# Two layer norms share their logarithm, exponential and shift, and the attention norm is applied on ScalarE instead of VectorE

## The reference

```python
h   = layernorm(x)                                # norm of x, no gamma
q   = h @ Wq.T + bq ; k, v = ctx @ Wk.T + bk, ctx @ Wv.T + bv
att = h + (q @ (k.T @ v, block by head)) / 4      # attention residual
x1  = x + layer_norm(att) * gamma + beta
h2  = layernorm(x1)                               # norm of x1
w, e = top2(softmax(h2 @ gate_w.T))
out = x1 + sum_i w_i * relu(h2 @ expert_w[e_i].T + expert_b[e_i])
```

## Time and profile before

| | |
|---|---|
| median of 3 runs | 878.47 us (875.46 to 879.29) |
| the profiled execution | 878.41 us, span 876.6 us |
| busy share of the span | PE 86%, DVE 78%, ACT 68%, POOL 67% |
| dense half, roughly | start to 478 us |
| expert half | 478 us to the end |

### The profile page before, as it was taken

The page is one execution under the profiler, slowest core; times in us unless marked ns, Lnnn a source line. Parts: engine busy times, 40 slices in busy tenths (PEclk is TensorE's granted clock), DMA queues, the critical chain, the costliest instruction groups (busy, mean ns, idle before and its releaser), DMA issues. The chain is left out here.

```text
span 876.6 us, 21081 instructions
## 1 busy us (share of the span) xinstructions
PE 754.3 (86%) x5513; PEld 658.7 (75%) x5514; DVE 684.4 (78%) x2226; ACT 592.4 (68%) x1660; POOL 590.6 (67%) x776
## 2 busy tenths in 40 slices
PE   5988899999999999999998877788768899877850
PEld 4866688888888888888884777787756799767750
DVE  4999999999999999999995766777763566555540
ACT  4877789989998998899982545555542567554540
POOL 4578766666666666666664667777675577777775
PEclk9999999999999999999999999999999999999985
DMA  7526456666667667667612889999986999999941
GB/s 226 175 69 176 143 181 215 213 228 227 203 231 234 202 221 236 212 204 233 225 45 86 284 295 305 308 303 305 317 278 226 312 402 373 326 313 306 309 170 73
DMA packets 137628, 205.79 MB, mean 235 GB/s; under 512 B 38962, under 2 KB 74290, under 8 KB 137546
## 3 DMA queue, kind: packets, MB, share of 16 engines
q1 hardware_dynamic: 113101, 130.72, 47.4%
q0 software_dynamic: 24448, 74.14, 22.9%
HBM read 87.99 MB, written 116.81 MB: 234 GB/s over the span
## 5 line engine op out<-in xcount | busy, mean ns | idle before, releaser
L627 POOL DMA_INDIRECT bins<-row_in,put_at x143 | 139.3, 974 | 61.0 <-issue 47.7
L627 POOL DMA_INDIRECT out_rows<-xh,put_at x143 | 138.9, 971 | 56.1 <-issue 37.7
L607 POOL DMA_INDIRECT bins<-rows x128 | 126.6, 989 | 71.0 <-POOL rows L600 47.5
L697 PE MATMUL ps_q<-h_t,wq 128*128 128x256 f32 x512 | 131.6, 379 | 0.0
L556 POOL TENSOR_TENSOR c_rest<-c_sb,c_head 128x240 fp32r<-128x240 f32 x64 | 44.4, 694 | 86.8 <-DVE x L1157 82.2
L697 PEld LDWEIGHTS ps_q<-h_t,wq 128*128 128x128 f32 x512 | 91.7, 189 | 13.2 <-ACT h_t L942 0.4
L990 ACT ACTIVATE ps_q<-ps_q,row_in 128x256 f32<-128x256 f32 x144 | 58.5, 444 | 56.8 <-PE ps_q L826 55.4
L824 PE MATMUL ps_q<-we_head,row_head 128*128 x288 | 87.9, 305 | 8.6 <-DVE row_rest L1288 8.5
L901 ACT ACTIVATE q_t<-ps_q,bq_sb 128x256 f32<-128x256 f32 x128 | 60.4, 472 | 34.5 <-PE ps_q L697 34.5
L571 POOL TENSOR_TENSOR x_beta<-xh,beta_sb 128x512 f32<-128x512 f32 x64 | 81.9, 1280 | 0.8 <-DVE x L1157 0.8
L825 PE MATMUL ps_q<-we_head,row_rest 128*128 x288 | 81.5, 283 | 0.0
(11 more groups left out here) (178 smaller groups left out, 2413.2 us busy)
## 6 DMA issues: line engine op xcount, KB each, us to landing
bins<-zeros SPq DMA_DIRECT2D x48, 768.0 KB, 4.6
row_in<-bins SPq DMA_DIRECT2D x128, 260.0 KB
row_in<-bins SPq DMA_DIRECT2D x160, 132.0 KB, 2.1
xh<-in_x SPq DMA_DIRECT2D x64, 256.0 KB, 2.7
c_sb<-in_ctx_t SPq DMA_DIRECT2D x64, 120.0 KB, 3.3
we<-in_we_t SPq DMA_DIRECT2D x8, 512.0 KB, 6.9
bins<-row_in,put_at POOLq DMA_INDIRECT x143, 3.7
out_rows<-xh,put_at POOLq DMA_INDIRECT x143, 4.6
```

The lines of the kernel that those rows point to most:

```text
L607: pool.indirect_dma_start(out=bins[0], in_=r[:, t, :], out_offset=bass.IndirectOffsetOnAxis(ap=r[:, t, POS_COL:POS_COL + 1].bitcast(I32), ...
L627: pool.indirect_dma_start(out=bins[1] if k == 0 else out, in_=row_in[:, t, :] if k == 0 else y[:, t, :], out_offset=bass.IndirectOffsetOnA ...
L697: mm = pe.matmul(ps_q[dc][:, 0:S], wq[:, c, dc * P:(dc + 1) * P], h_t[:, c, :, :], start=(c == 0), stop=(c == KC - 1))
```

## The change

The logarithms and exponentials of the norm of x (batch s+1) and of the attention residual (batch s-1) become one logarithm and one exponential on ScalarE (`inverse_roots_x_att`), which wait for both sets of moments. VectorE makes both shifts in one instruction (`mean_shifts`). ScalarE applies the norm to the attention residual, one instruction per tile (`normalise_attention`), and stands for that ahead of the copy of h2. VectorE then multiplies both tiles by gamma in one instruction and adds `x_beta` to both in one (`scale`, `finish_x1`); `scale` moves from ahead of the mask to the end of the step. The shift of the norm of x1 moves from two instructions on ScalarE to one on VectorE, between the top values and their indices.

```diff
-            def shift_of_x1(b):
-                act.wait_ge(s_rstd[2], b.times(1, 1))
...
-                for t in range(NT):
-                    a = act.activation(rows[:, b.buf(4), t, S_COL:S_COL + 1], st[:, 2, b.buf(2), t, 1:2], ACT.Identity,
-                                       bias=sigma[:, t:t + 1], scale=-1.0)
...
+            def inverse_roots_x_att(s):
+                norms, n = norms_of(s)
+                if (s + 1).exists():
+                    act.wait_ge(s_mv[0], (s + 1).times(1, 1))
+                if (s - 1).exists():
+                    act.wait_ge(s_mv[1], (s - 1).times(1, 1))
+                act.activation(lnv[:, norms], st[:, norms, n, :, 2], ACT.Ln, bias=eps[:, 0:1],
+                               scale=1.0 / D).then_inc(s_ln["x_att"], 1)
+                act.wait_ge(s_ln["x_att"], s.times(1, 2))
+                act.activation(rstd[:, norms, n, :], lnv[:, norms], ACT.Exp, scale=-0.5).then_inc(s_rstd["x_att"], 1)
+
+            def normalise_attention(b):
+                act.wait_ge(s_shift["x_att"], b.times(1, 3))
+                if b.c >= 1:
+                    act.wait_ge(s_x1, (b - 1).times(NT, NT))
+                for t in range(NT):
+                    a = act.activation(scaled[:, t, :], att[:, t, :], ACT.Identity,
+                                       bias=nmr[:, 1, t:t + 1], scale=rstd[:, 1, b.buf(2), t:t + 1])
+                a.then_inc(s_z, 1)
...
+            def mean_shifts(s):
+                norms, n = norms_of(s)
+                dve.wait_ge(s_rstd["x_att"], s.times(1, 2))
+                dve.scalar_tensor_tensor(out=nmr[:, norms], in0=st[:, norms, n, :, 1], scalar=-1.0,
+                                         in1=rstd[:, norms, n, :], op0=ALU.mult, op1=ALU.mult
+                                         ).then_inc(s_shift["x_att"], 1)
+
+            def shift_of_x1(b):
+                dve.wait_ge(s_sigma, b.times(1, 1))
+                if b.c >= 4:
+                    dve.wait_ge(s_row[b.buf(4)], (b - 4).uses(4, 32))
+                dve.tensor_tensor(rows[:, b.buf(4), :, S_COL], sigma[:], st[:, 2, b.buf(2), :, 1],
+                                  ALU.subtract).then_inc(s_shift["x1"], 1)
...
-                dve.wait_ge(s_mv[1], b.times(1, 1))
-                for t in range(NT):
-                    i = dve.scalar_tensor_tensor(out=scaled[:, t, :], in0=att[:, t, :],
-                                                 scalar=st[:, 1, b.buf(2), t, 1:2], in1=gamma_sb[:],
-                                                 op0=ALU.subtract, op1=ALU.mult)
-                i.then_inc(s_scaled, 1)
+                dve.wait_ge(s_z, b.times(1, 1))
+                dve.tensor_tensor(scaled[:], scaled[:], gamma_sb[:].unsqueeze(1).to_broadcast([P, NT, D]),
+                                  ALU.mult).then_inc(s_scaled, 1)
...
-                for t in range(NT):
-                    dve.scalar_tensor_tensor(out=x1[:, b.buf(2), t, :], in0=scaled[:, t, :],
-                                             scalar=rstd[:, 1, b.buf(2), t:t + 1],
-                                             in1=x_beta[:, b.buf(2), t, :], op0=ALU.mult,
-                                             op1=ALU.add).then_inc(s_x1, 1)
+                dve.tensor_tensor(x1[:, b.buf(2)], scaled[:], x_beta[:, b.buf(2)], ALU.add).then_inc(s_x1, NT)
```

More of the change, by code:

```diff
@@ L217, in build @@
         sigma = sb("sigma", [P, NT])
-        nmr = sb("nmr", [P, NT])
+        nmr = sb("nmr", [P, 2, NT])
         scores_top = sb("scores_top", [P, NT, E + 8])
@@ L300, in build @@
         s_mv = [sem(f"moments{n}_ready") for n in range(3)]
-        s_ln = [sem(f"log_var{n}_ready") for n in range(3)]
-        s_rstd = [sem(f"rstd{n}_ready") for n in range(3)]
-        s_nmr = {0: sem("shift0_ready"), 2: sem("shift2_ready")}
+        s_ln = {"x_att": sem("log_vars_x_attention_ready"), "x1": sem("log_var_x1_ready")}
+        s_rstd = {"x_att": sem("rstds_x_attention_ready"), "x1": sem("rstd_x1_ready")}
+        s_sigma = sem("sigma_x1_ready")
+        s_shift = {"x_att": sem("shifts_x_attention_ready"), "x1": sem("shift_x1_ready")}
+        s_z = sem("attention_normalised")
         s_h = sem("h_ready")
@@ L363, in batch_of, with norms_of @@
             return view[b.c]
+        def norms_of(s):
+            return slice(0 if (s + 1).exists() else 1, 2 if (s - 1).exists() else 1), (s + 1).buf(2)
         def pieces(step, each):
@@ L883, in _, with inverse_root_x1 @@
             act.activation(wkv_head[:], wkv, ACT.Copy).then_inc(s_wkvh, 1)
[L885 to L893, removed]
+            def inverse_root_x1(b):
+                act.wait_ge(s_mv[2], b.times(1, 1))
+                act.activation(lnv[:, 2, :], st[:, 2, b.buf(2), :, 2], ACT.Ln, bias=eps[:, 0:1],
+                               scale=1.0 / D).then_inc(s_ln["x1"], 1)
+                act.wait_ge(s_ln["x1"], b.times(1, 1))
+                act.activation(sigma[:], lnv[:, 2, :], ACT.Exp, scale=0.5).then_inc(s_sigma, 1)
+                act.activation(rstd[:, 2, b.buf(2), :], lnv[:, 2, :], ACT.Exp, scale=-0.5).then_inc(s_rstd["x1"], 1)
+            def inverse_roots_x_att(s):
[16 more added lines that the diff above has]
+                a.then_inc(s_z, 1)
             def copy_q(b, dc):
@@ L908, in gate_exps @@
                 act.activation(exps[:], gaps[:], ACT.Exp).then_inc(s_exp, 1)
-            def shift_of_x1(b):
-                act.wait_ge(s_rstd[2], b.times(1, 1))
-                if b.c >= 4:
-                    act.wait_ge(s_row[b.buf(4)], (b - 4).uses(4, 32))
-                for t in range(NT):
-                    a = act.activation(rows[:, b.buf(4), t, S_COL:S_COL + 1], st[:, 2, b.buf(2), t, 1:2], ACT.Identity,
-                                       bias=sigma[:, t:t + 1], scale=-1.0)
-                a.then_inc(s_nmr[2], 1)
             def shift_x1(b):
-                act.wait_ge(s_nmr[2], b.times(1, 1))
+                act.wait_ge(s_shift["x1"], b.times(1, 1))
                 for t in range(NT):
@@ L928, in normalise_x @@
             def normalise_x(b):
-                act.wait_ge(s_nmr[0], b.times(1, 1))
+                act.wait_ge(s_shift["x_att"], b.times(1, 1))
                 if b.c >= 4:
@@ L934, in normalise_x @@
                     a = act.activation(h[:, b.buf(4), t, :], x_sb[:, b.buf(4), t, :], ACT.Identity,
-                                       bias=nmr[:, t:t + 1], scale=rstd[:, 0, b.buf(2), t:t + 1])
+                                       bias=nmr[:, 0, t:t + 1], scale=rstd[:, 0, b.buf(2), t:t + 1])
                 a.then_inc(s_h, 1)
@@ L952, in step @@
                 if b.exists():
-                    inverse_root(2, b)
+                    inverse_root_x1(b)
                 if s.exists():
@@ L956, in step @@
                 if b.exists():
-                    shift_of_x1(b)
                     shift_x1(b)
-                if nxt.exists():
-                    inverse_root(0, nxt)
+                if nxt.exists() or p.exists():
+                    inverse_roots_x_att(s)
                 if f.exists():
@@ L963, in step @@
                 if p.exists():
-                    inverse_root(1, p)
+                    normalise_attention(p)
                 if b.exists():
@@ L1196, in step @@
                     top_values(f)
+                if b.exists():
+                    shift_of_x1(b)
                 if f.exists():
@@ L1211, in step @@
                     add_kv_bias(s)
-                if nxt.exists():
-                    mean_shift(0, nxt)
+                if nxt.exists() or p.exists():
+                    mean_shifts(s)
                 if f.exists():
                     pick_ranks(f)
-                if p.exists():
-                    scale(p)
-                if f.exists():
                     sum_exps(f)
@@ L1225, in step @@
                     first_weights(f)
+                if p.exists():
+                    scale(p)
                 if f.c == NB - 1:
```

1 line of the change is left out of this document (removed).

## The result

The changed kernel takes 922.0 us (median of 4 runs, 921.58 to 922.57); the kernel before, beside it on the same chip, takes 878.9 (875.46 to 880.0, 4 runs). The ratio is 1.0498, interval 1.0468 to 1.0528: **slower by 43 us**, where 919 was forecast. The profiled execution's span is 919.8 us against 876.6.

What follows compares the result with a forecast made beforehand. VectorE was taken to pace the dense half at 6.64 us a step. Terms -0.35 + 0.39 + 0.02 + 0.09 + 0.50 gave about 0.64 a step; 31.4 + 6.8 + 2.4 = 40.6 on 878.4 gave 919 us, range 892 to 927.

Steps and rivals of the forecast that it cites:

- case A: Whole kernel: the prediction's main case, all its terms as summed, 919 us, own range 908 to 925; chance 0.77.
- the weight steps and the ends: Dense half: seven steps with `we` work lose 0.97 each, 6.8 us; eight end steps 0.3 each, 2.4 us.
- the even steps: Middle of the dense half: 49 steps, each 0.64 us longer, 31.4 us in all.
- The shift is held: VectorE, dense step: the shift of x1, two SBUF inputs, is blocked until GpSimd's `x_beta` ends, +0.39 us a step.
- The late shared `rstd`: Dense step: VectorE waits after `kv` for ScalarE's shared logarithm and exponential, which need the attention's moments; +0.09 us.
- The hole in front of `kvm`: VectorE, dense step: with the scaled pair moved away, `kvm` waits idle for `ps_mg`, +0.50 us.
- The merged pairs: VectorE, dense step: two `scaled` and two `x` become two 512-column instructions of 0.69 us; -0.35 us a step.
- ScalarE hidden, 0.14 to spare: Dense step: ScalarE's normalisation runs from 4.62 to 5.70, is needed at 5.84, and adds no time.
- case D: Dense half: ScalarE becomes the pace, gate and attention late, 0.1 to 0.15 us a step above A, 926; chance 0.07.
- B: Dense half: the shift is not held, 0.23 us a step over 64 steps, 893 us; chance 0.09.
- C: Dense half: no hold and `kvm` does not wait, -0.26 us a step over 62 steps, 862 us; chance 0.04.
- E: Whole kernel: no change, as B with a hole of only a third, 880 us; chance 0.03.

Runs made afterwards that it cites:

- e1: The changed kernel with sigma kept in PSUM, so the shift of x1 reads one input from SBUF; 900.0 us, ratio 1.0248.
- e2: The kernel before with only the shift of x1 moved to VectorE, both inputs in SBUF; 899.7 us, ratio 1.0258.
- e3: The kernel before with only the shift of x1 moved to VectorE and sigma in PSUM; 880.1 us, ratio 1.0018.
- e6: The changed kernel with GpSimd's `x_beta` moved behind the scatters, sigma still in SBUF; 976.8 us, ratio 1.1123.
- e7: The kernel before with the row of expert numbers that `onehot` compares with kept in PSUM; 879.6 us, ratio 1.0026.
- e4: e1 with the attention norm back on VectorE in pairs and old places, logarithm, exponential and shift still shared; 891.0 us, ratio 1.0137.
- e5: e1 with the reciprocal, the place and the first weights moved in front of `kvm`; 899.2 us, ratio 1.0228.
- e8: e1 with the row of expert numbers that `onehot` compares with also kept in PSUM; 893.8 us, ratio 1.0181.

## Why the prediction was right, and what it mis-sized

**The result.** 919 forecast, 922.0 measured, inside case A's own range; the last 50 distances of `att` give 30.4 us (31.4 forecast for 49), the first thirteen 12.5 where 9.2 was forecast for the weight steps and the ends. So part of the closeness is luck: the even steps were forecast too dear and the others too cheap, and inside the even step two terms too large stand against two too small. With e1 in place of the change those thirteen cost 4.1, so 8.4 of the 12.5 is the hold, under `we_sum` and `we` too; the forecast gave it 0.73 in seven of them, 5.1 together. In the plain weight step both of its parts came out, 10.46 - 9.74 = 0.72 (0.73 forecast) and, in e1 against before, 9.74 - 9.48 = 0.26 (0.24). What it missed is that in three other steps the shift itself is held by `we`, for 1.85 to 2.23 us.

**The shift is held** (+0.39): right, and the main cause. Measured +0.34 in the trace, 0.31 by the change against e1, 0.32 by e2 against e3. It is less than forecast because the shift ends 0.02 behind `x_beta`, where the forecast had 0.07 (2.06 against 1.99). It goes with one input in PSUM, comes by itself in the kernel before, and goes when `x_beta` is elsewhere. The Trainium skill, SBUF — State Buffer, section Who interferes with whom, says that the second of two such instructions is blocked until the first is done; the rows agree, 0.02 us behind `x_beta` and 0.03 for `nmr` in e6, except that this `nmr` is marked as starting 0.16 ahead of `x_beta` and is held all the same. In e7 the hold outlasts the first and takes in the next, 3.59 us, of which the page says nothing.

**The late shared `rstd`** (+0.09): mis-sized; +0.15 in the trace, 0.17 by e4 against e3. The term took 0.57 us from the statistics' end to the end of Exp; it is 0.64 (335.35 to 335.99), as the logarithm starts 0.10 behind, not 0.04.

**The hole in front of `kvm`** (+0.50): +0.43. Counted from the statistics of x1, `kv` came 0.08 sooner than forecast, and so did `kvm` (5.14 for 5.23), as the hold was smaller; `nmr` came when forecast (4.42 for 4.44), as the logarithm was later. The hole lost that difference. Merged pairs and hole together are +0.14 (+0.15 forecast).

**The merged pairs** (-0.35): -0.29 (-0.20, and -0.09 for the wait that went). The durations were right (0.685 and 0.693 for 0.69), the wake-up was not: one to the next is 0.78 and 0.73 in place of 0.72 each.

**ScalarE hidden, 0.14 to spare**: the one step that failed. The normalisation was timed well (4.62 to 5.72 for 4.62 to 5.70), but `kvm` came 0.09 sooner, VectorE was at `scaled` at 5.75 instead of 5.84, and 0.03 is what is left. In the changed kernel this costs nothing on top, so case A held, but the hole isn't the sole price of the move: e5 took it away and gained nothing. Of case D, a lateness that adds time, there is none in the changed kernel, but ScalarE is level with the pace: the gate on TensorE waits for the copy of h2 in 47 steps between 127 and 480 us, 13.2 us in all.

**The sum by runs.** Hold 7.25 - 6.94 = 0.31; norm moved to ScalarE and products merged 6.94 - 6.80 = 0.14; sharing 6.80 - 6.63 = 0.17; shift on VectorE 6.63 - 6.64, nothing. Together 0.61, the step's difference.

**The other cases.** B forecast 893 for a shift that isn't held, 0.23 a step; e1 is that kernel, 900, and 0.30 a step. In it the shared `rstd` and the merged pairs cost 0.06 to 0.07 each more than forecast and the hole 0.06 less. That is 3 to 4 of the 7 us between; the rest wasn't taken apart. C fell: `kvm` waits. E fell with both. The clock stayed at 1.00 in the even stretch; with the weights it was 0.97 (1.00 before), and what that cost wasn't taken apart.

No kernel tried beats the one before; e3 equals it.

## What to carry to other kernels

Before an instruction goes to VectorE, look at which of its inputs are in SBUF and at what GpSimd does at that moment: a tiny one can cost what is left of GpSimd's large one, and one small operand in PSUM took that away (22 us here), whereas moving GpSimd's work in time only moved the collision. Freeing one held instruction can also bring the next one into the hold, as in e7. When two scalar steps are merged, the early result becomes as late as the late one; ask who waited for the early one. An instruction that looks like work may be the cover of a wait, and behind a filled hole a second chain may end at the same moment, so price every chain that ends there.

## What the runs showed that was not expected

- A held instruction can be held through two GpSimd instructions in a row: 3.59 us for `gaps`, which takes 0.17 alone (e7). In e8 it ended between the two four times (0.37 to 0.39) and behind the second once (2.83). How late it comes isn't the whole answer: there it came 0.47 us before the end of `we_sum`, while the shift of the changed kernel at 92.68 came 0.73 before it and still got out between the two. What decides that stays open.
- `nmr` in e6 is marked as starting at 325.73, 0.16 before `x_beta` at 325.89, and is still held to its end. Being first by the trace's starts doesn't save it.
- TensorE's granted clock fell to a mean of 0.80 in the stretch behind an idle time of 1.53 us (e6), and eight products took 1.89 us instead of 1.14; behind an idle time of 1.56 one step earlier it stayed at 1.00, and so it did in the changed kernel, whose waits are shorter.
